# A graph and mixture-of-experts kernel: three long VectorE operations issued in parts of 256 columns

## The reference, cut to what matters

```
x = x + L0_gnn(layernorm(x))      # two graph convolutions, edge weights, 106250 edges, 6250 nodes
x = x + L0_ffn(layernorm(x))      # 6 experts, top 2
x = x + L1_gnn(layernorm(x)):
    mish(x) = x * tanh(softplus(x))
    xn  = mish(nodes @ W_dense.T + b_dense)
    y   = mish(edge_features @ W_edge.T + b_edge)      # [106250, 256]
    msg = relu(xn[src] + y)
    agg = segment_sum(msg, dst)
    out = mish((xn + agg) @ W_out.T + b_out)
x = x + L1_ffn(layernorm(x))      # 8 experts, top 2
```

## Time and profile before

| | |
|---|---|
| median of 3 runs | 4279.02 us (4276.55 to 4279.75) |
| span of the profiled execution | 4272.1 us |
| GpSimd busy, of the span | 2823.4 us (66%) |
| TensorE / VectorE / ScalarE busy | 3514.0 / 2295.0 / 1939.7 us |
| gathers L509, 832 | mean 1056 ns |
| gathers L1110, 832 | mean 953 ns |
| gathers L1669, 832 | mean 1019 ns |

### The profile page before, as it was taken

One profiled execution on the slowest core, in us unless ns is written; L12 is line 12 of the kernel. 1 busy time (PEld: TensorE's weight loads), 2 busy tenths in 40 slices (PEclk: granted clock), 3 DMA queues, 4 the chain that ended last, 5 costly groups with the idle time before them and its releaser, 6 DMA issues. The chain is left out here.

```text
span 4272.1 us, 68475 instructions
## 1 busy us (share of the span) xinstructions
PE 3514.0 (82%) x17723; PEld 3093.3 (72%) x17723; DVE 2295.0 (54%) x6976; ACT 1939.7 (45%) x3024; POOL 2823.4 (66%) x2732
## 2 busy tenths in 40 slices
PE   4777777777756899999999968888888888649999
PEld 4666666666645788888888867777777777538887
DVE  6566556556554445545445436666666666632222
ACT  4455555555541333333333445555555555423333
POOL 3677777777767777766676227777777777353444
PEclk7788788888776999999999987777777787559999
DMA  6455555555543222222222126666666666534443
GB/s 177 154 187 188 179 174 183 178 180 178 178 140 107 69 68 66 69 66 64 68 67 64 36 96 208 212 206 212 209 209 208 212 211 191 172 137 92 98 98 60
DMA packets 287817, 605.53 MB, mean 142 GB/s; under 512 B 61999, under 2 KB 163342, under 8 KB 287499
## 3 DMA queue, kind: packets, MB, share of 16 engines
q1 hardware_dynamic: 166267, 344.34, 25.0%
q0 software_dynamic: 114784, 245.67, 21.0%
q10 hardware_dynamic: 6576, 13.36, 0.9%
HBM read 460.33 MB, written 144.67 MB: 142 GB/s over the span
## 5 line engine op out<-in xcount | busy, mean ns | idle before, releaser
L1669 POOL DMA_INDIRECT y_node<-node_table,src_sb x832 | 847.6, 1019 | 379.2 <-issue 378.9
L509 POOL DMA_INDIRECT conv_gath<-support_table,src_sb x832 | 878.4, 1056 | 284.3 <-issue 259.9
L1110 POOL DMA_INDIRECT x_gath<-hidden_table,src_sb x832 | 792.9, 953 | 353.6 <-issue 259.9
L664 PE MATMUL conv_pz<-conv_we,conv_edge 128*128 128x256 f32 x2240 | 643.1, 451 | 76.9 <-PEq L97 76.7
L1682 PE MATMUL y_pa<-y_hot,y_node 128*128 128x64 f32 x3328 | 523.6, 326 | 181.7 <-PEq L97 181.1
L1682 PEld LDWEIGHTS y_pa<-y_hot,y_node 128*128 128x128 f32 x3328 | 506.8, 240 | 214.7 <-issue 212.0
L664 PEld LDWEIGHTS conv_pz<-conv_we,conv_edge 128*128 128x128 f32 x2240 | 510.2, 234 | 170.2 <-issue 81.4
L655 PE MATMUL conv_ps<-conv_hot,conv_gath 128*128 128x64 f32 x1664 | 255.6, 305 | 213.5 <-DMA conv_gath<-support_table,src_sb 210.9
L655 PEld LDWEIGHTS conv_ps<-conv_hot,conv_gath 128*128 128x128 f32 x1664 | 242.5, 219 | 245.9 <-DMA conv_gath<-support_table,src_sb 238.5
L1734 ACT ACTIVATE y_node<-y_node 128x1024 f32<-128x1024 f32 x208 | 219.4, 1056 | 340.6 <-ACTq L97 340.1
L1692 PE MATMUL y_pz<-y_we,y_edge 128*128 128x256 f32 x1104 | 361.0, 499 | 13.0 <-PEq L97 13.0
(11 more groups left out here) (256 smaller groups left out, 5844.8 us busy)
## 6 DMA issues: line engine op xcount, KB each, us to landing
conv_edge<-in_edge_t SPq DMA_DIRECT2D x140, 512.0 KB
edge_mish_table<-conv_neg SPq DMA_DIRECT2D x140, 512.0 KB
y_neg<-edge_mish_table SPq DMA_DIRECT2D x139, 512.0 KB, 4.2
y_edge<-in_edge_t SPq DMA_DIRECT2D x69, 512.0 KB
e_rows<-expert_rows SPq DMA_DIRECT2D x56, 272.0 KB, 3.3
conv_gath<-support_table,src_sb POOLq DMA_INDIRECT x832
x_gath<-hidden_table,src_sb POOLq DMA_INDIRECT x832
y_node<-node_table,src_sb POOLq DMA_INDIRECT x832, 3.1
```

The lines of the kernel that those rows point to most:

```text
L509: pool.indirect_dma_start(gath[g % SLOTS][:, j, :], None, table[:, :], bass.IndirectOffsetOnAxis(ap=c.src[:, col:col + 1], axis=0),).then_ ...
L664: last = pe.matmul(ps_z[r % 2][:, j, :], edge[r][:, m, j * P:(j + 1) * P], we[:, m, :], start=m == 0, stop=m == KD - 1)
L1110: pool.indirect_dma_start(gath[g % SLOTS][:, j, :], None, table[:, :], bass.IndirectOffsetOnAxis(ap=c.src[:, col:col + 1], axis=0),).then_ ...
L1669: pool.indirect_dma_start(node[g % SLOTS][:, j, :], None, c.t3[:, :], bass.IndirectOffsetOnAxis(ap=c.src[:, col:col + 1], axis=0),).then_i ...
```

## The change: what it does

In both stages the clamp and the last product of mish are issued as four instructions of 256 columns instead of one of 1024, and the output's subtraction as two of 256 columns instead of one of 512. The semaphores stand behind the last of the parts, so nothing is released earlier or waited for more often. Elements, operands and results are the same, and no DMA changes. The bias additions (L523, L1784) stay whole, as do L1819, L1820 and L1825.

```
--- before.py
+++ after.py
@@ -522,11 +522,15 @@
 
                 link(dve, nc.vector.tensor_tensor(neg[r][:], ps_z[r % 2][:], bias[:].unsqueeze(1).to_broadcast([P, CG, D]), ALU.add), neg_own)
                 dve.sem_inc(z_free[r % 2], 1)
-                nc.vector.tensor_scalar(q[r][:], neg[r][:], ZMAX, None, ALU.min).then_inc(z_ready[r], 1)
+                for j in range(CG):
+                    last = nc.vector.tensor_scalar(q[r][:, j, :], neg[r][:, j, :], ZMAX, None, ALU.min)
+                last.then_inc(z_ready[r], 1)
 
             def mish_end(r):
                 take(dve, q_ready[r])
-                link(dve, nc.vector.scalar_tensor_tensor(neg[r][:], q[r][:], -1.0, neg[r][:], ALU.add, ALU.mult), neg_own)
+                for j in range(CG):
+                    last = nc.vector.scalar_tensor_tensor(neg[r][:, j, :], q[r][:, j, :], -1.0, neg[r][:, j, :], ALU.add, ALU.mult)
+                link(dve, last, neg_own)
                 dve.sem_inc(neg_ready[r], 1)
 
             def add(places, s):
@@ -1783,11 +1787,15 @@
                 dve.sem_inc(edge_free[r], 1)
                 link(dve, nc.vector.tensor_tensor(z[r][:], ps_z[r][:], bias[:].unsqueeze(1).to_broadcast([P, CG, D]), ALU.add), own)
                 dve.sem_inc(z_free[r], 1)
-                nc.vector.tensor_scalar(q[r][:], z[r][:], ZMAX, None, ALU.min).then_inc(z_ready[r], 1)
+                for j in range(CG):
+                    last = nc.vector.tensor_scalar(q[r][:, j, :], z[r][:, j, :], ZMAX, None, ALU.min)
+                last.then_inc(z_ready[r], 1)
 
             def mish_end(r):
                 take(dve, q_ready[r])
-                link(dve, nc.vector.scalar_tensor_tensor(z[r][:], q[r][:], -1.0, z[r][:], ALU.add, ALU.mult), own)
+                for j in range(CG):
+                    last = nc.vector.scalar_tensor_tensor(z[r][:, j, :], q[r][:, j, :], -1.0, z[r][:, j, :], ALU.add, ALU.mult)
+                link(dve, last, own)
 
             def message(k, i, s):
 
@@ -1826,7 +1834,9 @@
                 if to is ps_o:
                     dve.sem_inc(o_free, 1)
                 take(dve, xo_in[b], 16)
-                link(dve, nc.vector.tensor_tensor(x, x, now, ALU.subtract), own)
+                for s in range(2):
+                    last = nc.vector.tensor_tensor(x[:, s, :], x[:, s, :], now[:, s, :], ALU.subtract)
+                link(dve, last, own)
                 dve.sem_inc(xo_ready, 1)
 
             def step(k, i, places, before, begin=False, end=False):
```

## The result

The changed kernel takes 4241.6 us (median of 4 runs, 4238.1 to 4249.3) against 4279.4 us before in the same comparison: ratio 0.9915, 95% interval 0.9902 to 0.9929, some 36 us faster. 4180 us were forecast, and the range ended at 4222. The direction was right, and four tenths of the size came.

What follows compares the result with a forecast made beforehand. GpSimd's gathers in a row were taken to bound first aggregation and edge stage. Shorter stalls save 69.8 and 28.9 us, VectorE's cost counts nothing: 4279.0 - 98.7 = 4180 us, range 4150 to 4222.

Steps and rivals of the forecast that it cites:

- What bounds the kernel: First aggregation and edge stage: each lasts as long as 832 gathers in a row with a fixed gap.
- The hold model and its sum for the gathers: Streaming VectorE operations stall gathers at two touches; splitting saves 0.509 us a mish, 69.8 us first aggregation, 28.9 us edge stage.
- rivals 1 and 2: Gathers between parts: 1, none enters before the last, 4378 us (0.05); 2, only clamp gaps stay shut, 4273 us (0.07).
- first touch: Moment 0.13 us after a gather's start when a streaming clamp or two-SBUF-input operation can stop it; the second is at 0.82.
- What VectorE pays: Parts cost VectorE 0.51 us a mish, 71 us first aggregation, 35 us edge stage; costed at nothing, covered by idle time.
- Half a microsecond at the end of a stage: VectorE's delay at the end of a stage, taken to be within the rounding.
- another engine takes part of it: Rival 3: TensorE, busy 919 of 1115 us, holds the edge stage; its 28.9 us are lost, 4209 us (0.13, like losses included).

Runs made afterwards that it cites:

- e1: Changed kernel with the clamp whole again in both stages, product in four and subtraction in two kept: 4213.7 us, ratio 0.9844 to the kernel before.
- e2: Kernel before with only the clamp in four parts in both stages, product and subtraction whole: 4254.8 us, ratio 0.9944.
- e9: Kernel before with the product in two of 512 columns and the subtraction in two, clamp whole, both stages: 4219.4 us, ratio 0.9881.
- e10: Kernel before with only VectorE's run-time bound checks of table positions left out: 4237.8 us, ratio 0.9922.
- e6: Kernel before with six more 64-column VectorE products after each clamp of the first aggregation: 4377.5 us, ratio 1.0236.
- e7: Changed kernel with the clamp whole again in both stages and VectorE's bound checks left out: 4194.3 us, ratio 0.9804 to the kernel before.
- e5: Changed kernel with VectorE's run-time bound checks of table positions left out: 4170.0 us, ratio 0.9749 to the kernel before.

## Why the prediction was wrong

*What bounds the kernel: right.* GpSimd's row of gathers set both stages, and shortening them did shorten the kernel.

*The hold model and its sum for the gathers: right in size, with luck in it.* 972 ns forecast and 968 measured in the first aggregation; in the edge stage 984 and 994, 20.7 us of the 28.9. There L1812, the adds that the change doesn't touch, may meet the gathers at other places than before, and the same code of that stage scattered by 7 us between the profiled executions (1071.8 to 1079.2), more than the clamp's 4. In the first aggregation the parts come out singly too: the product's 46 us by e1, where 47 were forecast, the clamp's 18 by e2 (23 forecast). But e9 and e10 moved the stalls by 18 and 15 us against the model, so an agreement within 3 us is better than it can promise. Gathers do get in between overlapping parts, of the clamp too, so the rivals 1 and 2 were wrong: both means fell, and the gather at 605.41 lasts 0.94 us although four clamp parts run from 605.83 to 606.86. That a clamp holds a gather at its first touch was taken without a row; the gather at 606.65 shows it.

*What VectorE pays: right in size, wrong in cover. This is the step that failed.* "Its cover is VectorE's idle time, 484 and 391 us: 2 us in a step of 33" took the window less the busy time for room. Busy time counts none of the sequencer's work: in each step the position load and six checks, the loop's branch, and about 0.5 us in front of every add and half of the bias additions (the idle times in the brackets of the timeline). The room was about 2 us a step (e6), and two edits drew on it from both sides: the gathers' step fell from 32.8 towards 24 x (968 + 304) ns = 30.5 us, VectorE's stream rose from 30.7 by 4 x 0.46 towards 32.5 us, and they crossed. The mean step is 32.2 us; L410's load, 2.5 us on the mean before and 2.1 after, makes up the difference. I had weighed the 0.51 us against a room of 14 us at the old pace of the gathers. Even there the four mishes' 2.0 us would have taken all of the true room, and the shorter gathers took away another 2.3 us of the step.

*Its price.* 58.1 us of new waits and 10.7 us of tail, 69 us of the forecast 98.7. "Half a microsecond at the end of a stage" was wrong for what seems the same reason: VectorE is now behind when the last gather is done. What is left, 30 us, is what came (28.8 us between the spans); the smaller differences cancel.

*The rival "another engine takes part of it": right in kind, wrong in place.* It named TensorE in the edge stage, at 4209 us. It was VectorE in the first aggregation. The edge stage kept all that its gathers gave: they waited 0.3 us for slots before and after.

*The Trainium skill's "VectorE: DVE Perf Modes", section "The TRN2 errata — SBUF-src ops pay a fixed extra latency per instruction",* with its advice against short operations, spoke to this side of the trade. Its figure was too dear (an estimated 0.94 us a mish; measured 0.46), but what more instructions cost VectorE was what decided.

*The Trainium skill's "SBUF — State Buffer", section "Who interferes with whom":* the trace agrees that the clamp and the product hold a gather up (1.28 and 1.53 us), not on "for the whole instruction": gathers slip in between instructions whose records overlap (0.94 us at 605.41).

## What to carry to other kernels

An engine's idle time is room only after its sequencer's work is taken off: waits "<-DVEq L97" of a fixed 0.5 us and long gaps at a loop's head, with nothing late on another engine, are its own time. Adding known work to the engine in the kernel before (e6) measures the room in one run; use the mean of the steps, as lengths can alternate. When a change speeds up the engine that sets the pace and pays with another one, compare the two new lengths of a step with each other, and take the part of the edit with the best return first: here the product in four alone gave 66 us and the whole change 36.

## What was not expected of the hardware

Run-time checks of loaded positions cost VectorE 1.6 us a step in the first aggregation, and 15 to 22 us in the mixing stage (e7, e10, e5), where nobody had looked. An edit that leaves every hold as it is can move the gathers' stalls by 15 us (1056 to 1038 ns in e10), and in the first aggregation, though not in the edge stage, two holds of 512 columns cost no more than four of 256 (e9). It looks as if the stall were a matter of the operations' place as much as of their length where the gathers release them; no run sets the two apart. Clamp parts of 256 columns follow each other every 0.20 to 0.25 us (0.90 to 1.03 us for four), less than the 0.295 us that one lasts.
